# Two-layer model on one core: shift rows, prefetches and the fill of the routed attention regrouped

## The chip, the cores and the metric

The program runs on one core of one Trainium2 chip. TensorE (PE) does matrix products and transposes into PSUM, VectorE (DVE), ScalarE (ACT) and GpSimd (POOL) work on elements, SyncE (SP) issues DMAs. The metric is the device time of one execution in microseconds (us), and the figure shown is the median of several executions.

## The reference

The input is a batch of B = 8 sequences of S = 512 token numbers with a model width D = 192. The reference adds up five blocks on one residual stream: a token layer, a linear attention, a soft mixture of experts, a quantised attention, and a routed block (an attention and a mixture of eight experts). Both attentions that matter here have 12 heads of 16 numbers:

```python
# quantised attention
q, k, v = heads(fake_quant(x) @ fake_quant(w_qkv) + b_qkv)
attn = einsum('bhnd,bhmd->bhnm', fake_quant(q), fake_quant(k)) * hd ** -0.5
attn = fake_quant(softmax(attn, axis=-1))      # 8 bits, one scale for the whole tensor
out  = fake_quant(einsum('bhnm,bhmd->bhnd', attn, fake_quant(v))) @ fake_quant(w_proj) + b_proj
# the routed block's attention
attn = softmax(einsum('bhnd,bhmd->bhnm', q, k) * hd ** -0.5, axis=-1)
x    = x + einsum('bhnm,bhmd->bhnd', attn, v) @ proj_w + proj_b
```

The scale of a fake quantisation is the largest absolute value over 127. For `attn` it is the largest softmax value anywhere, so all row sums must be known before the first value can be rounded.

## The kernel before

The program is a list of stages, each a function that cuts its tiles out of one arena in SBUF: `embed_and_trace`, `linear_attention`, `soft_moe`, `quantised_attention`, `routed_attention`, `routed_experts`. A stage is a chain of `nc.Block`s. Inside a block every engine has its own written program, ordered by semaphores, and no engine leaves a block before all are through. Loops are either Python loops (the code is written out) or `Fori` loops that an engine turns itself. `Signal` is a semaphore with a count per batch; `Link` waits for the instruction just issued on its own engine.

Both attentions go over the scores twice, and both have a gap between the passes in which the shift of each row is made ready.

**Quantised attention.** The first pass (from L1616) forms per batch and head the scores of queries in rows, takes their maxima (`MXq`, L1658), and sums the exponentials (`RS`, L1673); 24 units of two row tiles per batch, on four pairs of PSUM banks. The block between the passes (L1680 to L1739) makes of sums and maxima one shift per row, `W_`: reciprocals of all sums and their maximum over all partitions (L1688, L1689, L1713), the logarithm (L1718), a multiply and subtract (L1694). `W_` is split into three bf16 parts in `BP`, batch by batch (L1698, L1703), transposed by 32 small transposes (L1728), copied to `BT` with 36 partitions (L1707), and each of its 36 partitions goes by a DMA of its own into a row of the query tile `QI` (L1738). `KI` has ones in the same rows, so the second pass's matmul subtracts the shift by itself. The second pass (L1742 on) needs K spread into `QM` and V in `VS`, two buffers by batch parity. SP asks for these after the rows have landed, four DMAs for K and one for V per batch (L1762, L1764). The second pass computes turned scores (L1781), exponentials (L1819), rounding (L1841) and the read-out (L1799).

**Routed attention.** To get fp32 accuracy out of bf16 products, Q and K are each split in three bf16 parts, and six pairs of parts are stacked in the contraction: `ST_[j][side]` has 6 x 16 = 96 rows (`KR`) and three more for the shift. The parts go to DRAM (`ra_parts`, L2100) and come back as stacks by 12 DMAs a batch (`load_stacks`, L2007 to L2012), two stack buffers by batch parity.
The first pass has a fill and then eight batches. The work on one batch's projections is cut into 14 `pieces` for TensorE: two `turn`s (L2117), eight `product`s (L2126), four `values` (L2136). The fill does all pieces of batches 0 and 1; after that every unit of scores of batch b (L2148) is followed by one piece of batch b + 2. ScalarE copies and splits, GpSimd subtracts (L2086, L2089), VectorE normalises rows (L2023) and takes the maxima of 24 units a batch (L2032). SP (L2093 to L2104) stores the parts of a batch and then loads its stacks as soon as the scores of the batch that held the buffer are through:

```python
for k in range(2):
    p2.wait(sp, b, k + 1)
    for n in range(3):
        dst = parts[bass.ds(b, 1)].rearrange("o k n f c s -> (o k) n c f s")[k, n]
        sp.dma_start(dst, PT[k][n]).then_inc(s_wr[k], 16)
prev(sp, u1, i, j)
for k in range(2):
    sp.wait_ge(s_wr[k], 16 * 3 * (b + 1) + 1)
    load_stacks(sp, b, j, ld[j], (k,))
```

The block between the passes (L2175 to L2211) negates the maxima (L2183), splits them in three parts (L2186, L2188) in a tile that GpSimd first fills with zeros (L2178), transposes (L2195), copies (L2203), and stores the rows to DRAM (`ra_shifts`, L2209). The second pass (L2213 on) loads per batch the stacks again, the shift rows from DRAM (L2233), and a copy of V (L2236). A batch is 12 steps: four score matmuls (L2250), two exponentials (L2313), four read-outs (L2288). After steps 1 and 3 TensorE projects a half of the batch before (L2263), which must wait for VectorE: copy of the read-out (L2347), shuffle, reciprocal, multiply (L2353).

## Time and profile before

| | |
|---|---|
| median of 3 executions | 2894.81 us (2891.12 to 2895.28) |
| profiled execution, its own time | 2868.81 us |
| its span | 2867.1 us |
| TensorE busy, share | 1967.8 us, 69% |
| VectorE busy, share | 1521.2 us, 53% |
| ScalarE busy, share | 1124.2 us, 39% |
| GpSimd busy, share | 312.9 us, 11% |
| mean granted TensorE clock | 0.768 of full |
| DMA, mean over the span | 88 GB/s |

The span is what the profile covers of its execution; 1.7 us of that execution's time lie outside it. The stages follow one another, so a share over the whole span mixes stages with different limits. The quantised first pass runs from about 1039 to 1335 us of the span, the second from 1386 to 1617; the routed first pass from 1674 to 1977 with its fill, the second from 2021 to 2271. The rows further down are places in time from these stretches.

### The profile page before, as it was taken

What the parts mean: (1) busy time and instruction counts of PE and PEld (TensorE: products, weight loads), DVE (VectorE), ACT (ScalarE), POOL (GpSimd) and SP (SyncE); (2) the same over time, 40 slices, a digit from 0 to 9 for tenths busy, and PEclk for the clock granted to TensorE, in tenths of its full rate; (3) what the DMA queues carried; (4) which work ended last, traced back from release to release, by engine and by line L of the source; (5) the groups of instructions that cost most, each with busy time, mean ns of one, the idle gap of its engine ahead of it and who ended that gap; (6) DMA issues with size and microseconds to landing.
All of it is one profiled execution on the core that took longest, in us unless ns stands there. A gap on an engine that the chain in (4) does not pass through costs nothing. (4 is left out here: it accounts for less than half of the span.)

```text
span 2867.1 us, 32319 instructions
## 1 busy us (share of the span) xinstructions
PE 1967.8 (69%) x9516; PEld 1035.9 (36%) x9538; DVE 1521.2 (53%) x2573; ACT 1124.2 (39%) x1862; POOL 312.9 (11%) x338
## 2 busy tenths in 40 slices
PE   4787788678873436664577648885799740999960
PEld 3645645353341100000111223321233340888850
DVE  4366378640026668886477738896477640111113
ACT  1102222231113579996588622220688410322210
POOL 4000000001110000000000042220000026000026
PEclk9899989777865655555799767775899755999985
DMA  3041100138930000000100048772898022455533
GB/s 71 11 137 39 42 17 22 54 146 311 411 151 11 0 15 11 11 11 2 36 26 29 1 77 114 105 105 30 117 111 109 3 95 79 174 200 209 202 105 107
DMA packets 140738, 251.39 MB, mean 88 GB/s; under 512 B 28762, under 2 KB 108251, under 8 KB 135628
## 3 DMA queue, kind: packets, MB, share of 16 engines
q1 hardware_dynamic: 128340, 225.99, 30.8%
q0 software_dynamic: 12304, 24.20, 2.9%
q8 instruction: 52, 0.85, 0.1%
q14 instruction: 42, 0.34, 0.0%
HBM read 194.69 MB, written 38.04 MB: 81 GB/s over the span
## 5 line engine op out<-in xcount | busy, mean ns | idle before, releaser
L1641 PE MATMUL ps<-arena 128*128 x376 | 194.3, 620 | 158.6 <-ACT ps L1673 96.0
L1673 ACT ACTIVATE ps<-ps,arena 128x512 f32<-128x512 f32 x384 | 291.8, 993 | 9.7 <-DVE arena L1652 9.7
L1658 DVE TENSOR_REDUCE arena<-ps 128x1024 f32 x192 | 234.4, 1224 | 47.9 <-PE ps L1641 46.5
L2032 DVE TENSOR_REDUCE arena<-ps 128x1024 f32 (+1 forms) x192 | 226.8, 1221 | 47.2 <-PE ps L2148 42.8
L1819 ACT ACTIVATE arena<-ps,arena 128x1024 f32<-128x1024 f32 x192 | 197.8, 1111 | 36.6 <-DVE arena L1841 27.3
L2313 ACT ACTIVATE arena<-ps 128x1024 f32<-128x1024 f32 x192 | 185.2, 1022 | 38.2 <-PE ps L2250 36.4
L2148 PE MATMUL ps<-arena 96*128 96x512 bf16 x384 | 159.7, 509 | 36.6 <-DVE arena L2032 23.6
L531 PE MATMUL ps<-arena 96*128 96x456 f32 (+1 forms) x512 | 176.5, 498 | 9.3 <-DMA arena<-arena 5.7
L2701 ACT ACTIVATE arena<-ps,arena 128x256 f32<-128x256 f32 x234 | 89.5, 481 | 235.9 <-PE ps L2666 235.9
L1841 DVE TENSOR_SCALAR arena<-arena 128x1024 bf16<-128x1024 f32 x192 | 130.8, 691 | 95.6 <-ACT arena L1819 79.0
L2718 DVE TENSOR_TENSOR arena<-ps,arena 128x384 f32<-128x384 f32 x39 | 21.7, 557 | 289.4 <-PE ps L2677 289.4
L1673 ACT ACTIVATION_READ_ACCUMULATOR ps<-ps,arena 128x1 f32 x384 | 171.6, 447 | 0.0
L2677 PE MATMUL ps<-arena 128*128 128x192 f32 x936 | 162.5, 331 | 0.7 <-DVE arena L2718 0.7
L2677 PEld LDWEIGHTS ps<-arena 128*128 128x128 f32 x936 | 151.0, 190 | 13.6 <-issue 13.6
L1781 PE MATMUL ps<-arena 128*128 (+1 forms) x370 | 117.3, 398 | 39.1 <-DMA arena<-arena 36.4
L1641 PEld LDWEIGHTS ps<-arena 128*128 128x128 bf16 x384 | 26.0, 112 | 326.3 <-ACT ps L1673 228.3
L2250 PE MATMUL ps<-arena 99*128 99x512 bf16 x384 | 103.2, 389 | 38.4 <-DMA arena<-arena 34.0
L531 PEld LDWEIGHTS ps<-arena 96*128 96x128 f32 x512 | 100.5, 205 | 76.6 <-issue 58.8
L2662 PE MATMUL ps<-arena 128*128 128x256 f32 x468 | 109.4, 384 | 0.9 <-ACT arena L2701 0.9
L1799 PE MATMUL ps<-arena 128*32 128x512 bf16 x384 | 77.5, 400 | 46.8 <-DVE arena L1841 38.6
L2288 PE MATMUL ps<-arena 128*32 128x512 f32 x768 | 103.5, 611 | 3.3 <-ACT arena L2313 3.3
L1204 DVE COPY arena<-ps 128x768 f32<-128x768 f32 x16 | 15.3, 957 | 159.9 <-PE ps L1246 159.9
(370 smaller groups left out, 3265.4 us busy)
## 6 DMA issues: line engine op xcount, KB each, us to landing
arena<-in_sm_w_dram SPq DMA_DIRECT2D x128, 576.0 KB
arena<-in_re_w_dram SPq DMA_DIRECT2D x39, 1252.0 KB, 5.7
arena<-ra_parts SPq DMA_DIRECT2D x192, 192.0 KB, 9.8
ra_parts<-arena SPq DMA_DIRECT2D x48, 192.0 KB, 2.5
routed_in<-arena SPq DMA_DIRECT2D x1, 7488.0 KB, 26.4
arena<-routed_in SPq DMA_DIRECT2D x39, 192.0 KB, 5.5
routed_out<-arena POOLq DMA_DIRECT2D x39, 192.0 KB, 2.3
arena<-la_xt SPq DMA_DIRECT2D x16, 384.0 KB, 3.3
```

Source lines behind the costliest of these rows:

```text
L531: ins = pe.matmul(ps[:, 2 * (t % 2) + bank, to:to + w], XTs[j][:, c, t * P:(t + 1) * P], Wx[:, kind, c, at:at + w], start=(c == 0), stop=( ...
L1641: ins = pe.matmul(ps[:, 2 * (n % 4) + t % 2, :], QM[j][:, h, t * P:(t + 1) * P], KI[:, b, h // HG, :], start=True, stop=True)
L1658: v.tensor_reduce(MXq[:, b, h, 2 * u:2 * u + 2], ps[:, 2 * (n % 4):2 * (n % 4) + 2, :], AX.X, ALU.max).then_inc(s_lk, 1)
L1673: ins = act.activation(bank, bank, ACT.Exp, bias=nb[n % 4][:, t % 2:t % 2 + 1], scale=c_exp, accum_out=RS[:, b, h, t:t + 1])
L1781: ins = pe.matmul(ps[:, 2 * (n % 3) + q, :], QM[j][:, h, c * P:(c + 1) * P], QI[:, bass.ds(b, 1), g, :].rearrange("p o s -> p (o s)"), sta ...
L1819: act.activation(PF[n % 2], ps[:, 2 * (n % 3):2 * (n % 3) + 2, :].rearrange("p a s -> p (a s)"), ACT.Exp, scale=c_exp).then_inc(pe_.sem, 1)
L1841: v.tensor_scalar(PB[n % 2], PF[n % 2], MAGIC, MAGIC, ALU.add, ALU.subtract).then_inc(rd.sem, 1)
L2032: v.tensor_reduce(MX[:, bass.ds(b, 1), 2 * (n % 2):2 * (n % 2) + 2, n // 2].rearrange("p o t -> p (o t)"), ps[:, 2 * (n % 2):2 * (n % 2) + ...
L2148: ins = pe.matmul(ps[:, t, :], ST_[j][0][0:KR, h, t * P:(t + 1) * P], ST_[j][1][0:KR, h, :], start=True, stop=True)
L2313: act.activation(PF[e // 2 % 2][:, 2 * (e % 2):2 * (e % 2) + 2, :], ps[:, 2 * (e % 3):2 * (e % 3) + 2, :], ACT.Exp, scale=HD ** -0.5).then ...
L2662: pe.matmul(unit(k), wr[:, k * P:(k + 1) * P], XT[j][:, 0, :], start=True, stop=False)
L2677: ins = pe.matmul(ps[:, 7, h * D:(h + 1) * D], HT[j][:, k, h * P:(h + 1) * P], wr[:, at:at + D], start=(k == 0), stop=(k == KH - 1))
```

## The change

Quantised attention. `RS` and `MXq` change their order to batch, row tile, head, and the heads are numbered so that the twelve heads of one partition group stand together (`at_head`). The largest reciprocal is formed as the reciprocal of the smallest sum. The split into parts is done for all batches at once, with the three parts innermost in `BP`. The copy to `BT` is divided: VectorE the first four batches, ScalarE the last four. Three parts of one head lie in neighbouring partitions of `BT` and go by one DMA, 12 instead of 36. SP asks for K and V of batches 0 and 1 at the start of the block between the passes.

Routed attention. The fill does the pieces of batch 0 alone; batch 0's units carry those of batches 1 and 2, two pieces after a unit; VectorE normalises batch 2 in the middle of batch 0's maxima. Maxima are written negated. After the loads of the last batch, SP loads the stacks of batch 0 for the second pass, once batch 6's scores are through. The block between the passes is gone: its work stands at the head of the second pass's block, without zero fill and negation, and shift rows go from `BT` straight into `ST_`, three DMAs a batch. V is read in place, so its copies and the DRAM tensor `ra_shifts` go. TensorE's and ScalarE's loops over the batches are written out, and the last two batches of VectorE's first pass become a loop.

```diff
-    RS, MXq = g3(P, [B, NH, T]), g3(P, [B, NH, T])
+    RS, MXq = g3(P, [B, T, NH]), g3(P, [B, T, NH])
+    VS = [OQ.rearrange("p g s -> p (g s)").rearrange("p (t h d) -> p t h d", t=T, h=NH),
+          g3(P, [T, NH, 32], BF16)]
+    at_head = lambda h: h % HG * NG + h // HG
...
-                                             scale=c_exp, accum_out=RS[:, b, h, t:t + 1])
+                                             scale=c_exp, accum_out=RS[:, b, t, at_head(h):at_head(h) + 1])
...
-    BP = g4(P, [B, T, 3, NH], BF16)
+    BP = TMP[:, S:S + 3 * B * T * NH // 2].bitcast(BF16).rearrange("p (n h k) -> p n h k", h=NH, k=3)
     BT = g4(3 * NH, [B, S], BF16)
-    W_ = TMP[:, 0:B * NH * T].rearrange("p (b h t) -> p b h t", b=B, h=NH)
+    W_ = TMP[:, 0:B * NH * T].rearrange("p (n h) -> p n h", h=NH)
+    rows = lambda a: a.rearrange("p b t h -> p (b t) h")
...
+    def spread(sp, b, j):
+
+        for q in range(HG):
+            sp.dma_start(QM[j][32 * q:32 * q + 32].rearrange("p (g j) s -> p g j s", j=HG)[:, :, q, :],
+                         KI[32 * q:32 * q + 32, b, :, :]).then_inc(km[j], 16)
+        sp.dma_start(VS[j], VI[:, b, :, :, :]).then_inc(km[j], 16)
...
-            l(v.reciprocal(W_, RS))
-            v.tensor_reduce(pmax, W_, AX.XYZ, ALU.max).then_inc(s_b, 1)
+            l(v.tensor_reduce(pmax, RS, AX.XYZ, ALU.min))
+            v.reciprocal(pmax, pmax).then_inc(s_b, 1)
...
             for k in range(3):
-                for b in range(B):
-                    ins = v.tensor_copy(BP[:, b, :, k, :], turned(W_, b))
-                    if b == B - 1:
-                        l(ins)
+                l(v.tensor_copy(BP[:, :, :, k], W_))
                 if k < 2:
-                    for b in range(B):
-                        ins = v.tensor_tensor(turned(W_, b), turned(W_, b), BP[:, b, :, k, :], ALU.subtract)
-                    l(ins)
+                    l(v.tensor_tensor(W_, W_, BP[:, :, :, k], ALU.subtract))
...
             v.wait_ge(s_bt, 1)
-            v.tensor_copy(BT.rearrange("p (u b) s -> p u (b s)", u=4),
-                          ps[0:3 * NH, 0:4, :].bitcast(BF16)).then_inc(s_bc, 1)
+            v.tensor_copy(BT[:, 0:4, :].rearrange("p (u b) s -> p u (b s)", u=2),
+                          ps[0:3 * NH, 0:2, :].bitcast(BF16)).then_inc(s_bc, 1)
...
+            act.wait_ge(s_bt, 2)
+            act.activation(BT[:, 4:8, :].rearrange("p (u b) s -> p u (b s)", u=2),
+                           ps[0:3 * NH, 2:4, :].bitcast(BF16), ACT.Copy).then_inc(s_bc, 1)
...
-                                       BP[:, b, t, :, :].rearrange("p k h -> p (k h)"), m.identb)
-            ins.then_inc(s_bt, 1)
+                                       BP[:, b * T + t, :, :].rearrange("p h k -> p (h k)"), m.identb)
+                if b % 4 == 3:
+                    ins.then_inc(s_bt, 1)
...
-            sp.wait_ge(s_bc, 1)
-            for k in range(3):
-                for h in range(NH):
-                    row = 32 * (h % HG) + HD + k
-                    sp.dma_start(QI[row:row + 1, :, h // HG, :], BT[k * NH + h:k * NH + h + 1, :, :]
-                                 ).then_inc(s_q, 16)
+            for j in range(2):
+                spread(sp, j, j)
+            sp.wait_ge(s_bc, 2)
+            for q in range(HG):
+                for g in range(NG):
+                    row, at = 32 * q + HD, 3 * (q * NG + g)
+                    sp.dma_start(QI[row:row + 3, :, g, :], BT[at:at + 3, :, :]).then_inc(s_q, 16)
...
-            sp.wait_ge(s_q, 16 * 3 * NH)
-            with sp.Fori(0, B // 2) as i:
+            with sp.Fori(1, B // 2) as i:
                 for j in range(2):
-                    b = 2 * i + j
                     prev(sp, av, i, j)
-                    for q in range(HG):
-                        sp.dma_start(QM[j][32 * q:32 * q + 32].rearrange("p (g j) s -> p g j s", j=HG)[:, :, q, :],
-                                     KI[32 * q:32 * q + 32, b, :, :]).then_inc(km[j], 16)
-                    sp.dma_start(VS[j], VI[:, b, :, :, :]).then_inc(km[j], 16)
+                    spread(sp, 2 * i + j, j)
...
-                        "p o t -> p (o t)"), ps[:, 2 * (n % 2):2 * (n % 2) + 2, :], AX.X, ALU.max).then_inc(mx.sem, 1)
-
-            def batch(b, ahead):
-                if ahead:
-                    norm(b + 2)
-                maxima(b, range(NU))
+                        "p o t -> p (o t)"), ps[:, 2 * (n % 2):2 * (n % 2) + 2, :], AX.X, ALU.max, negate=True
+                                    ).then_inc(mx.sem, 1)
 
             norm(0)
             norm(1)
-            with v.Fori(0, B - 2) as b:
-                batch(b, True)
-            batch(B - 2, False)
-            batch(B - 1, False)
+            maxima(0, range(6))
+            norm(2)
+            maxima(0, range(6, NU))
+            with v.Fori(1, B - 2) as b:
+                norm(b + 2)
+                maxima(b, range(NU))
+            with v.Fori(B - 2, B) as b:
+                maxima(b, range(NU))
...
+            u1.wait(sp, B - 2, NU)
+            load_stacks(sp, 0, 0, sl[0])
...
-            def batch(b, i, j, ahead):
-                pe.wait_ge(ld[j], 16 * NLD * (i + 1))
+            def batch(b, ahead):
+                pe.wait_ge(ld[b % 2], 16 * NLD * (b // 2 + 1))
+                rate = -(-len(ahead) // (NU - 2))
                 for n in range(NU):
-                    scores(b, j, n)
-                    if ahead and 0 < n <= len(pieces):
-                        piece, *which = pieces[n - 1]
-                        piece(b + 2, *which)
-
-            for b in range(2):
-                for piece, *which in pieces:
-                    piece(b, *which)
-            with pe.Fori(0, B // 2 - 1) as i:
-                for j in range(2):
-                    batch(2 * i + j, i, j, True)
-            batch(B - 2, B // 2 - 1, 0, False)
-            batch(B - 1, B // 2 - 1, 1, False)
-
...
-        def _(pool):
-            pool.memset(BPP, 0.0).then_inc(s_bz, 1)
-
-        @block.vector
-        def _(v):
-            l = Link(v, s_c)
-            l(v.tensor_scalar(M, M, -1.0, None, ALU.mult))
-            v.wait_ge(s_bz, 1)
-            for k in range(3):
-                l(v.tensor_copy(BP[:, :, k, :], M))
-                if k < 2:
-                    l(v.tensor_tensor(M, M, BP[:, :, k, :], ALU.subtract))
...
+                    scores(b, b % 2, n)
+                    if n:
+                        for to, (piece, *which) in ahead[rate * (n - 1):rate * n]:
+                            piece(to, *which)
+
+            for piece, *which in pieces:
+                piece(0, *which)
             for b in range(B):
-                for t in range(T):
-                    ins = pe.transpose(ps[:, b, 0:S // 2].bitcast(BF16)[:, t * P:(t + 1) * P],
-                                       BPP[:, b * T + t, :], m.identb)
-            ins.then_inc(s_bt, 1)
-
...
-            for b in range(B):
-                ins = act.activation(BT[:, b, :], ps[0:3 * NH, b, 0:S // 2].bitcast(BF16), ACT.Copy)
-            ins.then_inc(s_bc, 1)
-
-        @block.sync
-        def _(sp):
-            sp.wait_ge(s_bc, 1)
-            sp.dma_start(shifts.rearrange("b n s -> n b s"), BT).then_inc(s_sh, 16)
-            sp.wait_ge(s_sh, 16)
+                coming = {0: (1, 2)}.get(b, (b + 2,) if b + 2 < B else ())
+                batch(b, [(to, piece) for to in coming for piece in pieces])
...
-    VS = [g4(P, [T, NH, 2, HD]) for _ in range(2)]
     PF = [g4(P, [HG, S]) for _ in range(2)]
     OT, OS = g4(P, [NG, S]), g4(P, [NG, S])
+    BP, BT = g4(P, [B * T, 3, NH], BF16), g4(3 * NH, [B, S], BF16)
+    VT = V.rearrange("p b (t h n) -> p b t h n", t=T, h=NH)
...
+    NL2 = NLD + 3
...
-            with sp.Fori(0, B // 2) as i:
-                for j in range(2):
-                    b = 2 * i + j
-                    prev(sp, st, i, j)
-                    load_stacks(sp, b, j, sl[j])
-                    sp.dma_start(ST_[j][0][KR:KR + 3, :, :], shifts[bass.ds(b, 1)].rearrange(
-                        "o (k h) s -> (o k) h s", k=3)).then_inc(sl[j], 16)
-                    prev(sp, av, i, j)
-                    sp.dma_start(VS[j].rearrange("p t h k d -> p (t h k d)"),
-                                 V[:, bass.ds(b, 1), :].rearrange("p o n -> p (o n)")).then_inc(sl[j], 16)
+            def shift_rows(b):
+                for k in range(3):
+                    sp.dma_start(ST_[b % 2][0][KR + k:KR + k + 1, :, :], BT[NH * k:NH * k + NH, b, :]
+                                 ).then_inc(sl[b % 2], 16)
+
+            sp.wait_ge(s_b0, 1)
+            shift_rows(0)
+            shift_rows(1)
+            load_stacks(sp, 1, 1, sl[1])
+            sp.wait_ge(s_bc, 2)
+            for b in range(2, B):
+                prev(sp, st, b // 2, b % 2)
+                load_stacks(sp, b, b % 2, sl[b % 2])
+                shift_rows(b)
...
+            pe.wait_ge(s_c, 5)
+            turned = ps[0:3 * NH, 0:4, :].bitcast(BF16)
+            for b in range(B):
+                for t in range(T):
+                    at = b % 2 * S + t * P
+                    ins = pe.transpose(turned[:, b // 2, at:at + P],
+                                       BP[:, b * T + t, :, :].rearrange("p k h -> p (k h)"), m.identb)
+                if b in (1, 3, B - 1):
+                    ins.then_inc(s_bt, 1)
+            pe.wait_ge(s_b0, 1)
+            pe.wait_ge(s_bc, 2)
...
                         ins = pe.matmul(ps[32 * q:32 * q + 32, 6 + (j + g) % 2, :],
-                                        VS[j][:, c_, h, :, :].rearrange("p k d -> p (k d)"), PF[n % 2][:, q, :],
+                                        VT[:, b, c_, h, :], PF[n % 2][:, q, :],
...
-            batch(0, 0, 0, False)
-            with pe.Fori(0, B // 2 - 1) as i:
-                batch(2 * i + 1, i, 1, True)
-                batch(2 * i + 2, i + 1, 0, True)
-            batch(B - 1, B // 2 - 1, 1, True, False)
+            for b in range(B):
+                batch(b, b % 2, b > 0, b + 1 < B)
...
-            with act.Fori(0, B) as b:
+            act.wait_ge(s_bt, 3)
+            act.activation(BT[:, B // 2:B, :].rearrange("p (u b) s -> p u (b s)", u=2),
+                           ps[0:3 * NH, 2:4, :].bitcast(BF16), ACT.Copy).then_inc(s_bc, 1)
+            for b in range(B):
...
+            shift = Link(v, s_c)
+            for k in range(3):
+                shift(v.tensor_copy(BP[:, :, k, :], M))
+                if k < 2:
+                    shift(v.tensor_tensor(M, M, BP[:, :, k, :], ALU.subtract))
+            for u, done in enumerate((s_b0, s_bc)):
+                v.wait_ge(s_bt, u + 1)
+                v.tensor_copy(BT[:, 2 * u:2 * u + 2, :].rearrange("p b s -> p (b s)"),
+                              ps[0:3 * NH, u, :].bitcast(BF16)).then_inc(done, 1)
```

## Rows read from the trace of the kernel before

**Rows 1.** Window: busy PE, PEld, DVE, ACT, POOL; granted clock, DMA share, GB/s.
```profile
1352.00:1378.00 26.00, 0.00 (x0) 0.00 (x0) 0.00 (x0) 0.00 (x0) 0.00 (x0) 0.50 0.05 11
```

**Rows 2.** Timeline between the quantised passes, one row later: start, us, engine, line, operation.
```profile
1334.94 2.55 DVE L1688 RECIPROCAL arena<-arena 128x384 f32<-128x384 f32 x1 [3.71 <-PEq L1616]
...
1340.14 0.97 DVE L1698 CAST arena<-arena 128x48 bf16<-128x48 f32 x8
...
1341.14 1.26 DVE L1703 TENSOR_TENSOR arena<-arena 128x48 f32<-128x48 f32 x8
...
1349.46 2.28 DVE L1707 COPY arena<-ps 36x4096 bf16<-36x4096 bf16 x1 [3.76 <-PE ps L1728]
...
1351.77 26.02 SPq L1738 DMA_DIRECT2D arena<-arena  x36
...
1379.40 3.08 SPq L1762 DMA_DIRECT2D arena<-arena  x4
...
1385.80 2.34 PE L1781 MATMUL ps<-arena 128*128 128x512 bf16 x5 [36.38 <-DMA arena<-arena]
...
1618.97 0.16 DVE L1355 RECIPROCAL arena<-arena 128x1 f32<-128x1 f32 x1
```

**Rows 3.** Timeline between the two passes of the routed attention.
```profile
1976.95 3.67 DVE L2183 TENSOR_SCALAR arena<-arena 128x384 f32<-128x384 f32 x1 [0.41 <-PEq L2014]
...
1980.66 0.36 DVE L2186 CAST arena<-arena 128x384 bf16<-128x384 f32 x1
...
1981.05 0.56 DVE L2188 TENSOR_TENSOR arena<-arena 128x384 f32<-128x384 f32 x1
...
1983.05 3.60 PE L2195 MATMUL ps<-arena 128*128 128x128 bf16 x32 [7.76 <-DVE arena L2186]
...
1986.68 3.95 ACT L2203 ACTIVATE arena<-ps 36x512 bf16<-36x512 bf16 x8 [77.22 <-PE ps L2195]
...
2002.62 19.21 SPq L2012 DMA_DIRECT2D arena<-ra_parts  x12
...
2020.67 2.74 PE L2250 MATMUL ps<-arena 99*128 99x512 bf16 x6 [34.02 <-DMA arena<-arena]
...
2023.11 3.77 ACT L2313 ACTIVATE arena<-ps 128x1024 f32<-128x1024 f32 x4
```

**Rows 4.** Timeline of the first pass's fill and of its batch 0.
```profile
1679.18 9.87 PE L2126 MATMUL ps<-arena 97*96 97x512 f32 x16 [1.62 <-ACT arena L2056]
...
1693.25 3.98 DVE L2023 TENSOR_SCALAR arena<-arena 128x192 f32 x4 [14.41 <-PE ps L2117]
...
1717.60 1.89 PE L2148 MATMUL ps<-arena 96*128 96x512 bf16 x4 [9.16 <-DMA arena<-ra_parts]
...
1725.32 24.24 DVE L2032 TENSOR_REDUCE arena<-ps 128x1024 f32 x20 [1.26 <-PE ps L2148]
...
1727.16 0.60 PE L2148 MATMUL ps<-arena 96*128 96x512 bf16 x2
...
1727.59 1.02 PE L2126 MATMUL ps<-arena 96*96 96x512 f32 x2
...
1728.45 0.59 PE L2148 MATMUL ps<-arena 96*128 96x512 bf16 x2
...
1748.37 5.65 SPq L2012 DMA_DIRECT2D arena<-ra_parts  x12
```

**Rows 5.** Timeline of the first pass's last units.
```profile
1969.48 7.07 DVE L2032 TENSOR_REDUCE arena<-ps 128x2 f32<-128x1024 f32 x6
```

**Rows 6.** Timeline of batch boundaries in the second pass.
```profile
2048.55 1.28 ACT L2313 ACT_TABLE_LOAD   x1
...
2078.13 1.28 ACT L2313 ACT_TABLE_LOAD   x1
...
2085.22 2.22 PE L2263 MATMUL ps<-arena 128*128 128x192 f32 x12 [0.69 <-DVE arena L2353]
...
2107.71 1.28 ACT L2313 ACT_TABLE_LOAD   x1
```

More of the change, by code:

```diff
@@ L1769, in _ @@
             av.start(pe)
-            pe.wait_ge(s_q, 16 * 3 * NH)
+            pe.wait_ge(s_q, 16 * NG * HG)
             def unit(n):
@@ L1946, in routed_attention @@
     ps, ra = m.ps, m.wk[1]
-    parts, shifts = io.ra_parts, io.ra_shifts
+    parts = io.ra_parts
     sem = lambda name: SEMS.new(nc, name)
@@ L2004, in routed_attention @@
     ld = [sem(f"ra_stacks{j}_loaded") for j in range(2)]
+    sl = [sem(f"ra_q_k_shift{j}_loaded") for j in range(2)]
     NLD = 2 * len(PAIRS)
     def load_stacks(eng, b, j, done, sides=(0, 1)):
+        one = slice(b, b + 1) if isinstance(b, int) else bass.ds(b, 1)
         for k in sides:
             for n, pair in enumerate(PAIRS):
-                src = parts[bass.ds(b, 1)].rearrange("o k n f (j d) s -> (o k) n d (f j) s", d=HD)[k, pair[k]]
+                src = parts[one].rearrange("o k n f (j d) s -> (o k) n d (f j) s", d=HD)[k, pair[k]]
                 eng.dma_start(ST_[j][k][HD * n:HD * n + HD, :, :], src).then_inc(done, 16)
@@ L2215, in routed_attention @@
     PF = [g4(P, [HG, S]) for _ in range(2)]
     OT, OS = g4(P, [NG, S]), g4(P, [NG, S])
+    BP, BT = g4(P, [B * T, 3, NH], BF16), g4(3 * NH, [B, S], BF16)
+    VT = V.rearrange("p b (t h n) -> p b t h n", t=T, h=NH)
+    M = MX.rearrange("p b t h -> p (b t) h")
+    s_c, s_bt, s_b0, s_bc = (sem(f"ra_shift_{n}") for n in ("chain", "turned", "first_copied", "copied"))
     NS = NG * T
@@ L2221, in routed_attention @@
     s_l3 = sem("ra_out_chain")
-    sl = [sem(f"ra_q_k_v{j}_loaded") for j in range(2)]
-    NL2 = NLD + 2
+    NL2 = NLD + 3
     with nc.Block(no_gpsimd_drain=True) as block:
@@ L2265, in project, with batch @@
                 ins.then_inc(pr.sem, 1)
-            def batch(b, i, j, behind, ahead=True):
+            def batch(b, j, behind, ahead=True):
                 for n in range(NS):
```

30 lines of the change are left out of this document (7 added, 23 removed).

## Prediction, made before the changed kernel was run

> **What bounds the kernel now.** I read the page first. Its chain that ended last covers only 2% of the span, so it says nothing here. The 40 slices say more: the busy digits and the granted clock sink together between the quantised passes and again between the routed passes, so these are two places where hardly anybody is at work. I then took windows and the timeline around both, SP's own timeline for the DMA queue, and last the boundaries between batches inside the passes.
>
> First gap, between the quantised passes: VectorE starts at 1334.94 and the first score of the second pass at 1385.80, 50.9 us in a row of single steps [rows 2]. The window shows every engine at zero for 26 us, TensorE's clock at its lower level (0.50), while SP issues 36 one-row DMAs, with the DMA engines 5% busy [rows 1]: the cost is the issuing, not the bytes. Only when the last row has landed does SP ask for K and V of the next pass, another 6.4 us (1379.40 to 1385.80) [rows 2].
>
> Second gap, between the routed passes: the last maxima end at 1976.55 [rows 5], the first exponential starts at 2023.11 [rows 3]. The sums before SP may ask for anything take until 1990.6, then the shift rows go out to DRAM, then the stacks come in; TensorE waits 34.0 us for a DMA [rows 3].
>
> Inside the routed first pass VectorE sets the pace: 1.21 us a unit of 1024 maxima, 24 units a batch [rows 4]. Its fill ends at 1717.60, when TensorE has been waiting 9.16 us for the stacks of batch 0, not for its own work [rows 4]. In the second pass a batch takes 29.58 us (2078.13 to 2107.71) [rows 6].
>
> **The change, part by part.** Sums are made in the profiled execution: 2868.81 us, with a span of 2867.1. The median shown is 2894.81, 26.0 higher. The edits take out waits and instructions of fixed length, so I subtract the same microseconds from the median; scaling them by 1.009 would move half a microsecond.
>
> *Quantised gap.* (a) The reciprocal of all 384 sums (2.55) becomes a minimum, at the price of the maximum it replaces, and a reciprocal of one element (0.16): 2.4 less [rows 2]. The logarithm moves up with it, to 1336.4; its table load of 1.28 (the length in [rows 6]) starts with the gap and is over by 1336.2. (b) Split into parts: 24 casts and 16 subtractions in groups of eight, 3 x 0.97 and 2 x 1.26, 5.6 with gaps [rows 2], become three casts and two subtractions of 384 elements. The routed stage has just these at 0.36 and 0.56 [rows 3], so 2.35; written with a step of three elements perhaps 0.1 more each. Gain 2.5 to 3.2, taken 2.9. (c) The 2.28 copy out of PSUM is halved. VectorE's half lies under the transposes; ScalarE's half, 36x2048, starts when they end. Eight copies of 512 take 3.95 [rows 3], 0.49 each, so at most 1.98: 0.3 less. (d) Rows: 36 DMAs in 26.02, 0.72 each; 12 are 8.7, or 9.2 at the 0.77 of the K spreads (3.08 for 4) [rows 2]. 17.3 less. Each now carries three partitions. If only three DMA engines serve such a DMA, each gets 96 KB. Of the old transfers 288 packets kept 16 engines busy 5% of 26 us, 0.072 us a packet [rows 1]; 96 packets on one engine are 6.9 us, still under the issuing, and only the last one's tail grows by 0.5. So 16.8; if a packet costs twice that, 13.8 us on three engines, it is 11.7. The Trainium skill, in "DMA: Bandwidth & Descriptors", section on why a DMA increments its semaphore by 16, says that the engine count is the largest up to 16 that divides the slowest dimension of both sides: eight before, three now. No row here shows which engines were used; this rule speaks against the edit and is the reason for the 0.5. (e) K and V of batches 0 and 1 are now asked for at the gap's start: 8 x 0.77 and 2 x 0.6 of SP's time, over by about 1342, and SP isn't wanted until about 1346. 6.4 less. What hides it is VectorE's and TensorE's chain of 11 us; without that cover it costs 7.4. The landing time of the last row, 1.6 (1377.79 to 1379.40) [rows 2], stays. Sum of (a) to (e): 28.8, bounds 23 to 30.
>
> *Short fill.* Before, the 14 pieces of batch 1 (2 transposes, 8 products, 4 of values) ran while the stacks of batch 0 were on their way, and TensorE still waited 9.16 us. Their removal from the fill makes nothing earlier: SP's stores and loads of batch 0 depend on batch 0 alone. The first score stays at 1717.6. But now these pieces come into batch 0, two to a unit. A pair of score matmuls is 0.43 (1727.16 to 1727.59), a product piece 0.86 (1727.59 to 1728.45) [rows 4]. Before, a unit was 1.29, near VectorE's 1.21, and the scores of batch 0 were done when SP asked again at 1748.37, 30.8 us [rows 4]. After: unit 0 is 0.9, units 1 to 14 are 14 x (0.43 + 2 x 0.86) = 30.1, units 15 to 23 are 9 x 1.21 = 10.9, and the first four units at half clock (1.89 for four matmuls at the start [rows 4]) add 1.6: 43.5. Turns and values are lighter than products; the two waits for ScalarE behind a transpose fill that up. So 12.7 later, and no later batch has slack to win it back. The stacks of batch 1: in the fill, from the last product (1679.18 + 9.87 = 1689.05) to their use took 28.5 us [rows 4]. Its products now end near 1731, so 1759.5, just inside the 1761 at which batch 0 ends. What is late next, if they miss it, is batch 1 itself, by 1 to 4 us. The normalisation of batch 2 now falls where GpSimd subtracts, and in such a place it took 3.98 for four [rows 4]: up to 2.7 more. I take 13, bounds 9 to 19. Negated maxima cost nothing in the reduction. Batches 6 and 7 go into a loop: 1.212 a unit in the loop, 1.178 out of it (24.24/20, 7.07/6) [rows 4, 5], 48 x 0.034 = 1.6 more.
>
> *Routed gap.* The negation (3.67, beside a memset of GpSimd's that goes too) leaves 2.4 of casts and subtractions, to 1979.4. The transposes take 3.6 [rows 3], to 1983.0. ScalarE's half of the copy, 1.95 at most, to 1985.0. VectorE copies the first two batches' quarter from about 1980.5, in some 0.6; three row DMAs of batch 0 follow at SP's 0.47 (5.65/12) [rows 4], issued by 1982.7, landed at the 1.6 of [rows 2] by 1984.3, at 4 us by 1986.7. Stacks of batch 0 are asked for when batch 6's scores end, 24 units of 1.178 or 28 us before the gap [rows 5]; the slowest issue of such a load here took 19.2, with another in front of it [rows 3]. The load of batch 1's stacks starts near 1984 behind six row DMAs and lands near 2001; it is wanted 27 us after the start. So the first score is at 1985.0 for 2020.67, and the table load no longer stands behind it, 1.3 less: the exponential at 1986.5 for 2023.11. 36.6 less, bounds 33 to 37.
>
> *Loops written out.* ScalarE's loop reloads its table once a batch, 1.28 [rows 6]; seven go. But TensorE cannot pass the projection of the batch before, and that waits for VectorE (0.69 idle at 2085.22, released by L2353) [rows 6], whose chain of copy, shuffle, reciprocal and multiply starts at the last read-out and does not see the table. ScalarE and TensorE come 1.28 earlier to a wait of 0.69, which becomes 1.97. Gain 0; if none of that held, 9. The Trainium skill, "ScalarE: Activation LUTs", section on what ACT_TABLE_LOAD costs, gives 1283 ns and a drain, 2.66 us a switch: the trace agrees on the load, shows no drain ahead of it, and by that price the most would be 18.6.
>
> Sum: -28.8 + 13 + 1.6 - 36.6 = -50.8. 2868.8 becomes 2818.0, and the median 2894.8 becomes 2844.0.
>
> **Rivals.** *The fill is free:* the stacks of batch 0 land sooner without batch 1's work beside them, or ScalarE's and VectorE's share sets the pace. For it: DMA and engines did run together there. Against: those loads were a plain transfer with nothing of batch 1 in front. Sum -63.8: 2831. *The table loads count:* -59.8, 2835. Against: the projection wait. *Something new waits:* rows on three engines 5, stacks of batch 1 missing their time 4, the GpSimd collision 2.7; together -39: 2856. *The prefetch doesn't get through:* batch 0 of the second routed pass waits for its stacks as before; 19 us of the 36.6 are lost, 2863. The stacks' buffer is free at batch 6's end, so I see nothing for it. *Slower than before:* TensorE's code for both routed passes is now written out, 16 batches. If reading it held TensorE up, under a DMA load that fills these stages, the change would turn at 50.8/16 = 3.2 us a batch; at 5 us it would end at 2924. Against: TensorE's old loop turns at every second batch, and its neighbouring batches take the same 29.58 (2048.55 to 2078.13 to 2107.71) [rows 6], so nothing shows that reading code costs; no row prices it for straight code.
>
> **How the numbers follow.** Forecast as summed 0.55, free fill 0.10, table loads 0.10, new waits 0.15, prefetch lost 0.05, slower 0.03, elsewhere 0.02. The likeliest case alone spans 2836 to 2852 by its bounds; with the neighbours the range is 2828 to 2860. A difference under 0.2% (6 us) can't be told from none: faster 0.95, same 0.02, slower 0.03.
>
> **What would show it.** From the last exponential of the first quantised pass to the first score of the second: about 22 us, with 12 row DMAs in 9. The first routed score after the fill as late as before, after a TensorE wait of 26 us, and batch 0 some 43 us long. From the last maxima to the first exponential about 10 us. A second-pass period still 29.6, with TensorE's wait ahead of L2263's projection near 2. I am wrong if batch 0 stays near 31, if the period falls to 28.3, or if either gap keeps a wait for a DMA of more than 3 us.

## Result and profile after

The changed kernel takes 2853.39 us (median of 4 executions, 2846.80 to 2857.18), the kernel before 2894.06 beside it: 40.7 us less, ratio 0.9859, 95% interval 0.9838 to 0.9879. The forecast, 2844.0, was 9 us too low; its range, 2828 to 2860, holds the time. The profiled executions are 2868.81 us before and 2854.61 after. Their difference is too small by 26 us, because that of before was 25 us under its median, in stages that the change doesn't touch: the quantised gap began at 1334.94 in it and at 1346.25 in that of after, and from the last exponential to the end it took 611.5 us and then 624.4. The change isn't the reason: in the changed kernel's later trace, beside which the kernel before took 2869.69 us, the two are 1335.26 and 609.3, and that execution takes 2828.48 us, 40.3 under the profiled one of before. So I compare stretch by stretch.

| stretch | before | after | difference | forecast |
|---|---|---|---|---|
| quantised gap: VectorE's start to first score of the second pass | 50.86 | 24.07 | -26.8 | -28.8 |
| quantised second pass and the way to the routed fill | 289.81 | 291.78 | +2.0 | 0 |
| routed fill: first transpose to first score | 41.99 | 42.55 | +0.6 | 0 |
| routed first pass: first score to last maxima | 258.95 | 276.03 | +17.1 | +14.6 |
| routed gap: last maxima to first exponential | 46.56 | 10.24 | -36.3 | -36.6 |
| routed second pass: first to last exponential | 232.46 | 237.58 | +5.1 | 0 |
| sum | | | -38.3 | -50.8 |

The sum lies within the interval of the difference of the medians, which is 35 to 47 us. The second row, on which the forecast has no word, is small and steady: 291.7 to 292.3 us in all ten traces here with the quantised part of the change, 289.8 and 290.1 in the two without it. Its cause is open. A stretch of one trace is not exact, the routed first pass least of all: with the same code it took 271.3 to 276.0 us in six traces.

The timeline of after in the quantised gap, which answers to [rows 2]:

```profile
1346.20 2.66 SPq L1693 DMA_DIRECT2D arena<-arena  x4
1346.20 1.28 ACT L1726 ACT_TABLE_LOAD   x1 [0.32 <-PEq L1619]
1346.25 0.55 DVE L1701 TENSOR_REDUCE arena<-arena 128x1 f32<-128x384 f32 x1 [3.72 <-PEq L1619]
...
1349.07 0.49 DVE L1710 CAST arena<-arena 128x384 bf16<-128x384 f32 x1
...
1349.59 0.56 DVE L1712 TENSOR_TENSOR arena<-arena 128x384 f32<-128x384 f32 x1
...
1355.21 1.87 ACT L1728 ACTIVATE arena<-ps 36x2048 bf16<-36x2048 bf16 x1 [6.90 <-PE ps L1739]
1357.10 9.76 SPq L1752 DMA_DIRECT2D arena<-arena  x12
...
1370.32 1.91 PE L1786 MATMUL ps<-arena 128*128 128x512 bf16 x4 [15.15 <-DMA arena<-arena]
```

The work up to the copy's end (1357.08) takes 10.8 us for 16.8, as forecast (6.0 less for 5.6). From there to the first score 13.2 us pass, and the forecast has 10.8: 8.7 of issuing (12 x 0.72, since its 17.3 is 26.02 less 8.7), 0.5 and 1.6 for the tail. The twelve rows take 9.8, 0.81 each, and from the last issue (1366.86) to the first score it is 3.5. These 2.4 less the 0.4 gained before are the miss of 2.0.

The timeline of the fill and batch 0, the routed first pass, against [rows 4]:

```profile
1685.23 5.79 SPq L2019 DMA_DIRECT2D arena<-ra_parts  x12
...
1704.65 1.89 PE L2157 MATMUL ps<-arena 96*128 96x512 bf16 x4 [26.09 <-DMA arena<-ra_parts]
```

TensorE waits 26.09 us where it waited 9.16, the forecast's 26, and the first score is no earlier. Its own rows go on:

```profile
1709.87 3.70 PE L2135 MATMUL ps<-arena 97*96 97x512 f32 x4 [0.77 <-ACT arena L2063]
...
1714.21 3.02 PE L2135 MATMUL ps<-arena 97*96 97x512 f32 x4
1717.07 0.59 PE L2157 MATMUL ps<-arena 96*128 96x512 bf16 x2
1717.50 1.88 PE L2135 MATMUL ps<-arena 97*96 97x512 f32 x4
1719.22 0.59 PE L2157 MATMUL ps<-arena 96*128 96x512 bf16 x2
...
1753.13 1.89 PE L2157 MATMUL ps<-arena 96*128 96x512 bf16 x4 [3.33 <-DMA arena<-ra_parts]
```

From 1717.07 a unit with two pieces is the forecast's 2.15 (1717.07 to 1719.22). Before that products run in 3.70 and 3.02 instead of 1.88: after 26 us of idleness TensorE starts at the lower of its clock levels (the granted clock from 1704.65 to 1717.07 is 0.52, where 0.50 is 1.2 GHz). Batch 0's scores end at 1749.8, 45.1 us after the first for the 43.5 forecast, and then TensorE waits 3.33 for the stacks of batch 1. SP's row for these:

```profile
1732.21 5.99 SPq L2019 DMA_DIRECT2D arena<-ra_parts  x12
```

From 1732.21 to their use is 20.9 us. The collision of batch 2's normalisation with GpSimd did not come: its four instructions took 1.24 us together.

So batch 0 takes 48.5 us in this trace, but this is the longest of six. Its window here, and in the run with the table loads back, whose first pass is the same code:

```profile
1704.65:1753.13 48.48, 40.44 (x129) 18.23 (x129) 31.07 (x32) 16.69 (x28) 16.79 (x8) 0.78 0.55 83
1703.31:1746.02 42.71, 36.03 (x129) 17.21 (x129) 29.50 (x28) 16.70 (x28) 16.80 (x8) 0.90 0.59 94
```

The work is the same, the granted clock is 0.78 here and 0.90 there, and the wait for the stacks of batch 1 is 3.3 us here and 0.9 there. Batch 1 took 31.0 us here for 34.0 before, and the forecast had allowed no later batch to win anything back.

Batches 6 and 7, whose maxima are now in VectorE's loop, took 60.7 us (1919.94 to 1980.68) for 57.7 (1918.89 to 1976.55). Their units:

```profile
1951.12 19.60 DVE L2039 TENSOR_REDUCE arena<-ps 128x1024 f32 x16 [0.18 <-PE ps L2157]
```

That is 1.225 us a unit (19.60/16) for the 1.178 of [rows 5] out of the loop. The negation isn't the reason: in the kernel before, too, such units start 1.14 and 1.32 us apart by turns in the loop and 1.14 and 1.21 out of it.

The timeline of the routed gap, for [rows 3]:

```profile
1981.35 0.36 DVE L2305 CAST arena<-arena 128x384 bf16<-128x384 f32 x1 [0.67 <-PEq L2021]
...
1983.74 3.60 PE L2219 MATMUL ps<-arena 128*36 128x128 bf16 x32 [4.43 <-DVE arena L2305]
1984.89 1.46 DVE L2310 COPY arena<-ps 36x1024 bf16<-36x1024 bf16 x2 [1.21 <-PE ps L2219]
1985.60 5.08 SPq L2196 DMA_DIRECT2D arena<-arena  x6
...
1987.38 1.87 ACT L2289 ACTIVATE arena<-ps 36x2048 bf16<-36x2048 bf16 x1 [76.88 <-PE ps L2219]
...
1989.26 1.28 ACT L2295 ACT_TABLE_LOAD   x1
...
1989.87 3.57 PE L2232 MATMUL ps<-arena 99*128 99x512 bf16 x8 [2.54 <-DMA arena<-arena]
...
1990.92 3.77 ACT L2295 ACTIVATE arena<-ps 128x1024 f32<-128x1024 f32 x4 [0.38 <-PE ps L2232]
```

The stacks have come; what TensorE waits 2.54 us for are the shift rows of batch 0, at 0.85 us an issue (5.08/6) instead of the 0.47 taken.

The second pass is where the forecast of nothing failed. TensorE's timeline at the first two boundaries, for [rows 6]:

```profile
2023.27 3.83 PE L2245 MATMUL ps<-arena 128*128 128x192 f32 x12 [1.86 <-DVE arena L2344]
...
2030.92 2.22 PE L2245 MATMUL ps<-arena 128*128 128x192 f32 x12
...
2054.61 2.22 PE L2245 MATMUL ps<-arena 128*128 128x192 f32 x12 [1.86 <-DVE arena L2344]
...
2060.59 1.73 PE L2245 MATMUL ps<-arena 128*128 128x192 f32 x9
```

The wait grew from 0.69 to 1.86, near the 1.97 forecast, at every boundary. But behind it the same twelve matmuls take 3.83 us once and 2.22 another time, and to the next projection it is 7.65 or 5.98 us. The windows behind the two waits (the columns of [rows 1]) show why:

```profile
2023.27:2031.00 7.73, 7.73 (x37) 4.50 (x37) 2.89 (x6) 3.34 (x4) 0.00 (x0) 0.78 1.15 122
...
2054.61:2060.60 5.99, 5.99 (x37) 2.92 (x37) 3.03 (x6) 3.27 (x4) 0.00 (x0) 1.00 1.16 127
```

The granted clock, the column after the five engines, is 0.78 behind the first wait, which mixes both levels (1.2 and 2.4 GHz), and 1.00 (2.4 GHz) behind the second. In this profile three of seven boundaries are of the slow kind: ScalarE is idle 5.68 us in them and 4.00 in the others. 3 x 1.68 = 5.0 is the +5.1. Before, with a wait of 0.69, the clock stayed at 1.00.

### The profile page after: what moved, and what is told of

Its sections match the earlier page's. It is cut to its first block and busy times, and to the rows that moved or that the text cites. A ratio compares the mean times of both kernels' runs of the same rounds, so it can differ in the third digit from the quotient of the medians.

```text
span 2852.9 us, 31531 instructions
## 1 busy us (share of the span) xinstructions
PE 1960.8 (69%) x9516; PEld 1034.2 (36%) x9538; DVE 1512.6 (53%) x2539; ACT 1115.3 (39%) x1849; POOL 307.2 (11%) x337
```

## Experiments

Each ratio is to the kernel before on the same chip, whose medians were 2870.54 for the first four, 2891.78 for the next four and 2869.69 for the last two. Where an expectation names microseconds, it mostly counts from the changed kernel's 2853 beside a kernel before of 2894; on a chip where the kernel before takes 2870 the ratio is what to compare. The theory after the result: the missing ten microseconds are row DMAs and their landing (2), the short fill (2.5) and TensorE's lower clock in the second pass (5).

**The old fill in the changed kernel** (VectorE's loop over batches with it; TensorE's part is shown):

```diff
-            for piece, *which in pieces:
-                piece(0, *which)
+            for b in range(2):
+                for piece, *which in pieces:
+                    piece(b, *which)
             for b in range(B):
-                coming = {0: (1, 2)}.get(b, (b + 2,) if b + 2 < B else ())
+                coming = (b + 2,) if b + 2 < B else ()
```

> The changed kernel with the old fill: all 14 pieces of batches 0 and 1 before the first score, one piece a unit after that. Theory: the short fill alone made the first routed pass longer (from first score to last maxima 276.0 us in the changed kernel, 259.0 before). Then the first score stays about 42.3 us after the first transpose, batch 0 lasts 31 to 32 instead of 48.5 us, there is no wait of 3.3 us for the stacks of batch 1, and the time is some 16 us under the changed kernel, near 2837. Rival: the loops written out or the vector engine's new loop are to blame, and the first pass stays at 274 to 276 us, the time at 2853.

Measured: 2815.77 us, ratio 0.9801 (0.9787 to 0.9814), 0.0058 or 16.8 us of 2894 better than the changed kernel; with both intervals that is 10 to 24. The first pass took 260.2 us for 276.0. Its first score:

```profile
1696.37 1.89 PE L2154 MATMUL ps<-arena 96*128 96x512 bf16 x4 [10.72 <-DMA arena<-ra_parts]
```

The wait in front is 10.72 us: the work in the fill lay in the shadow of the transfer. The short fill is a loss. Over all traces here its first pass averages 273.8 us (six), that of the changed kernel's loops with the old fill 261.5 (three: this one and the two runs with both edits below): 12.3 us, so 276.0 against 260.2 is the upper end of the price. Batches 6 and 7 stay at 60.2 us in each of these three, so VectorE's loop costs 2.6 us of its own and the forecast had 1.6.

**The projection later.** Moved from after steps 1 and 3 to after steps 2 and 3, so that VectorE's chain has a step more.

```diff
-                    if behind and n in (1, 3):
-                        project(b - 1, 1 - j, n // 2)
+                    if behind and n in (2, 3):
+                        project(b - 1, 1 - j, n - 2)
```

> The changed kernel with the two halves of the projection after steps 2 and 3 of the next batch instead of 1 and 3. Theory: in the second routed pass the wait for the vector engine's chain sets the period (29.6 us with and without table loads), 1.86 us of TensorE waiting at each boundary, and after three of seven such waits the granted clock fell to half for the projection. One step (1.96 us) later the wait is over: period 28.0 to 28.6, no projection at half clock, 8 to 12 us less than the changed kernel, near 2843. Rival: ScalarE's exponentials set the period and the wait only moves to the second half or to the bank of the read-outs: period 29.3 to 29.6, gain under 3 us.

Measured: 2809.60 us, ratio 0.9785 (0.9772 to 0.9799). The second pass fell from 237.6 to 220.2 us, 17.4 less and more than expected. TensorE's waits before the projection are 0.31 us at most. Two windows of 192 us over most of the second pass show what has gone. The changed kernel's:

```profile
2021.00:2213.00 192.00, 178.98 (x1054) 65.70 (x1051) 132.77 (x182) 144.38 (x150) 0.00 (x0) 0.97 0.64 72
```

The window of the kernel with the later projection:

```profile
2008.00:2200.00 192.00, 190.10 (x1156) 65.69 (x1148) 146.20 (x200) 158.31 (x164) 0.00 (x0) 1.00 0.64 72
```

TensorE is busy 190.1 of 192 us, at a granted clock of 1.00: now it is the bound. What the 17.4 are made of is taken apart by the last runs.

**ScalarE's loop written out in the kernel before**, nothing else:

```diff
-            with act.Fori(0, B) as b:
+            for b in range(B):
```

> The kernel before with one edit: ScalarE's loop over the batches of the second routed pass written out, so seven table loads of 1.28 us go. Theory: they lay beside the wait for the vector engine. From first to last exponential the pass stays at 232.5 us, or gets up to 5 us longer where TensorE's longer wait (0.69 becomes 1.9) lets the granted clock fall; against the kernel before 0.999 to 1.002. Rival: the loads were on the path, 9.0 us less, 0.997.

Measured: 2872.77 us, ratio 1.0006 (0.9997 to 1.0016). The seven loads of 1.28 us are gone and nothing is won: by the ratio it is 1.7 us more, with an interval from 0.9 less to 4.6 more. Its boundaries are those of the changed kernel, of both kinds:

```profile
2051.82 2.22 PE L2263 MATMUL ps<-arena 128*128 128x192 f32 x12 [1.85 <-DVE arena L2353]
...
2081.43 3.54 PE L2263 MATMUL ps<-arena 128*128 128x192 f32 x12 [1.86 <-DVE arena L2353]
```

So the slower boundaries, four of seven here, come from this edit: in its trace the second pass is 238.3 us for 232.5. That the executions as a whole got slower by it is not shown, since the interval holds 1.

**The quantised part alone** in the kernel before (its diff as shown for that attention).

> The kernel before with the quantised attention's part of the change alone. Theory: its gap shrinks from 50.9 to about 24.1 us, as in the changed kernel, 26.8 less, and nothing else moves: 0.9907 of before, 2867. Rival: part of that is given back later, because the clock or the transfers behind it differ: under 22 us.

Measured: 2844.11 us, ratio 0.9907 (0.9892 to 0.9922), 26.4 us less, beside the 26.8 of the stretch with its 2.4 us more behind it (292.2 for 289.8). This part does alone what it does in the whole change, the small loss behind the gap included.

**Old fill and later projection together.**

> The changed kernel with both edits, the old fill (first pass 16 us shorter in its trace) and the projection after steps 2 and 3 (second pass 17 to 21 us shorter). Theory: the two lie in different passes and add. Ratios so far, against the kernel before on the same chip: 0.9801 and 0.9785, with the changed kernel at 0.9859 on its own chip; together 0.9785 - 0.0058 = 0.973, near 2792 where before is 2870. Rival: a pass that starts earlier loses what it gained at its first stacks or at the clock: 0.977 or more.

Measured: 2822.04 us, ratio 0.9751 (0.9730 to 0.9771), between the two numbers, and the interval holds both. The trace decides for adding up: the first pass takes 262.2 us, 13.8 less than in the changed kernel, and the second 220.1, 17.5 less. These 31.3 us make 0.9751 of 0.9859; the expected 0.973 was too low because it took 16.8 for the fill.

**The same, with the rows from two queues:** six of the twelve row DMAs are issued by ScalarE; the calls are shown.

```diff
+            act.wait_ge(s_bc, 2)
+            place_rows(act, (2, 3))
...
             sp.wait_ge(s_bc, 2)
-            for q in range(HG):
-                for g in range(NG):
-                    row, at = 32 * q + HD, 3 * (q * NG + g)
-                    sp.dma_start(QI[row:row + 3, :, g, :], BT[at:at + 3, :, :]).then_inc(s_q, 16)
+            place_rows(sp, (0, 1))
```

> The kernel of the run above, and the twelve three-row DMAs of the quantised gap issued half by SP and half by ScalarE. They take 9.7 us of issuing from SP alone, 0.81 each, and the last row is usable about 3 us after its issue. Theory A, each DMA's issue sets the pace: two queues need 4.9, the first score of the second quantised pass follows about 8 us after the copies in place of 12.8, 4.9 us less. Theory B, few DMA engines carry all rows and are the limit (96 packets each at 0.072 us or more, 6.9 us or more, and a tail): 9 to 12 us, so 1 to 4 us less. Against the run above 0.998 to 1.000.

Measured: 2818.48 us, ratio 0.9736 (0.9714 to 0.9757), the fastest version here against its own kernel before; its interval overlaps that of the run before it, the trace decides:

```profile
1355.33 4.92 SPq L1702 DMA_DIRECT2D arena<-arena  x6
1355.33 5.80 ACTq L1702 DMA_DIRECT2D arena<-arena  x6
...
1364.31 2.32 PE L1792 MATMUL ps<-arena 128*128 128x512 bf16 x5 [10.92 <-DMA arena<-arena]
```

From the end of the copy to the first score 9.0 us, 12.9 in the run before it. The issue takes 5.8 for 9.8, since ScalarE needs longer for its six (5.80) than SP (4.92), and the tail behind the last issue stays at 3.2 (3.1 in the run before). The 3.9 us are fewer than theory A's 4.9 and within theory B's 1 to 4, so the number alone doesn't part them; that the first score follows the end of the issuing by the same time in both speaks for A. The tail has a part of each. In the changed kernel's trace the semaphore updates, which no view prints, put the landing of the first of the twelve 2.1 us behind its issue and of the last 3.0; the one-row DMAs of before landed 1.3 us behind theirs, first and last alike. So 0.9 us of the tail is growth over the twelve; why a single row of three partitions takes 0.8 longer than one of one is open.

**The table loads back in the changed kernel:** only ScalarE's loop as before.

> The changed kernel with ScalarE's loop over the batches of the second routed pass kept as a loop, so that a table load of 1.28 us comes back seven times (TensorE's code stays written out). Theory: TensorE then waits 0.7 us instead of 1.9 for the vector engine before the projection, and its granted clock does not fall there: no projection at half clock, every batch boundary with ScalarE idle 2.8 us beside a load of 1.28, and from first to last exponential 231 to 233 us instead of the 237.6 of the changed kernel: 5 us less in spite of the added work. Rival: written-out code of TensorE itself costs those 5 us, or the loads are on the path after all: 237 to 246 us.

Measured: 2847.85 us, ratio 0.9842 (0.9821 to 0.9862), which overlaps with the changed kernel's interval. In the trace the second pass took 233.2 us for 237.6. ScalarE's rows at two boundaries:

```profile
2041.83 1.28 ACT L2295 ACT_TABLE_LOAD   x1
2043.12 5.65 ACT L2295 ACTIVATE arena<-ps 128x1024 f32<-128x1024 f32 x6
2051.68 3.90 ACT L2295 ACTIVATE arena<-ps 128x1024 f32<-128x1024 f32 x4 [2.91 <-PE ps L2232]
...
2071.40 1.28 ACT L2295 ACT_TABLE_LOAD   x1
2072.69 5.65 ACT L2295 ACTIVATE arena<-ps 128x1024 f32<-128x1024 f32 x6
2081.25 3.90 ACT L2295 ACTIVATE arena<-ps 128x1024 f32<-128x1024 f32 x4 [2.91 <-PE ps L2232]
```

With seven loads of 1.28 us more the pass is shorter: every boundary is of the fast kind, TensorE's wait is 0.77, and its projection takes 2.22. An eighth load stands before the first exponential and makes the gap 1.4 us longer (11.6 for 10.2), so 3.0 of the 4.4 us are left. The pass is also within 0.7 us of the 232.5 of before, so TensorE's written-out code costs no more than that.

**Without the early ask for batch 0's stacks:** the load goes out at the head of the gap.

```diff
-            u1.wait(sp, B - 2, NU)
-            load_stacks(sp, 0, 0, sl[0])
...
+            load_stacks(sp, 0, 0, sl[0])
             sp.wait_ge(s_b0, 1)
```

> The changed kernel without the one early step: the stacks of batch 0 for the second routed pass are asked for at the head of the gap, where SP is free, instead of during batch 7 of the first pass. Theory: 12 loads under no other load need 16 to 17 us from the first issue, and the row DMAs follow them in the queue: first score about 18 us after the gap's start instead of 8.5, 9 to 11 us more than the changed kernel. Rival (the forecast's price for a lost prefetch): 19 us more. Rival: nothing, since the shift rows set the moment.

Measured: 2867.51 us, ratio 0.9908 (0.9889 to 0.9926), 14 us more than the changed kernel. From the end of ScalarE's copy to the first exponential 16.2 us instead of 1.7. Timeline:

```profile
1990.59 13.00 SPq L2019 DMA_DIRECT2D arena<-ra_parts  x12
...
2003.13 3.15 PE L2231 MATMUL ps<-arena 99*128 99x512 bf16 x7 [17.03 <-DMA arena<-arena]
```

The load was issued from 1979.79 and the score stood until 2003.13, 23.3 us, with batch 1's stacks issued in between; the early ask works, and is worth 14 to 15 us, between the 9 to 11 and the 19 named for it. The 9 to 11 had counted 16 to 17 us for the load; it took 23.3.

**The changed kernel again, and the later projection with the table loads back.** Two runs on one chip, to take the 17.4 us apart.

> The changed kernel as it is, beside the next run on the same chip, as the measure for it. Expected ratio to the kernel before 0.986, as measured for it, within 0.002. In its second routed pass some of the seven boundaries show a wait of TensorE for VectorE of 1.86 us and then the projection's twelve matmuls in more than 3 us instead of 2.22; if the granted clock decides by chance of timing, the number of such boundaries may differ from the three seen before.

> The changed kernel with two edits: the projection of the batch before is put behind the third and fourth step of the next batch instead of the second and fourth, and ScalarE's loop of the second routed pass is a loop again, so its table load of 1.28 us stands in each batch. It tells apart where the 17.4 us of the later projection came from. Theory A: the projection's wait was the only cover of the table loads, and with the wait gone they count in full; the period goes from 27.9 to 29.2, the second pass from 220.2 to about 229, ratio 0.9785 + 0.0031 = 0.982. Theory B: the later projection moves the end of the batch for another reason and something else still covers the loads: period 27.9, ratio within 0.001 of 0.9785. In both no projection runs at the lower clock.

Measured: 2830.84 us, ratio 0.9863 (0.9848 to 0.9878), and 2817.96 us, ratio 0.9822 (0.9808 to 0.9836), which is theory A's 0.982; its interval keeps theory B's 0.9785 out. In the trace of the changed kernel five of seven boundaries were of the slow kind this time, and its second pass took 241.0 us. ScalarE's rows of the other:

```profile
2004.36 1.28 ACT L2295 ACT_TABLE_LOAD   x1
...
2015.33 1.94 ACT L2295 ACTIVATE arena<-ps 128x1024 f32<-128x1024 f32 x2 [2.07 <-PE ps L2232]
...
2033.16 1.28 ACT L2295 ACT_TABLE_LOAD   x1
...
2044.13 1.94 ACT L2295 ACTIVATE arena<-ps 128x1024 f32<-128x1024 f32 x2 [2.07 <-PE ps L2232]
```

Periods are 28.8 us and the pass 225.7. So from 237.6 or 241.0 us: the clock's share is what the loads back alone give, 4.4 to 7.8; putting the projection later gives 7.5 more (233.2 to 225.7); only then do the loads count, 5.5 us (225.7 to 220.2), 0.8 a batch and not theory A's full 1.28. By traces the loads cost 6.9 us with the 1.4 in the gap; the ratios say 10.6, and their intervals allow 5 to 16.

## Why the prediction came out as it did

The signs and the places were right: two gaps gained, one price paid. What was off were sizes, and one term taken at nothing, which is a step that failed although the time lies in the range.

- *Quantised gap, -28.8: measured -26.8.* (a) to (c) were right within 0.4 us. (d) took 0.72 a row in its sum (8.7 for the twelve) where it is 0.81, and a tail of 1.6 + 0.5 where it is 3.5. As (d) assumed, issuing is the larger part of the time: dividing it between two queues gave 3.9 us. (e) held: nothing of K and V is late. The sign "a wait for a DMA of more than 3 us in either gap" came true by the letter (15.15 us here), but the forecast's own sum has 10.8 us of rows in that wait, so as a sign it was badly made.
- *Quantised second pass, no term: measured +2.0,* in every trace with this part of the change.
- *Short fill and loop, +13 + 1.6: measured +17.1, +0.6 in the fill.* Of the 17.1 batches 6 and 7 have 3.1, where the loop's 1.6 was taken from a mean of units (1.212 and 1.178) that the loop's own units of 1.225 exceed. Batches 0 to 5 have 14.0, near the 13, but by luck in this trace: batch 0 was 5.0 too long (1.6 in the scores, mostly the start at half clock, for which the sum has 1.6 already, and 3.3 for the stacks of batch 1, "just inside", a lateness that the text names as 1 to 4 and didn't add), and batches 1 to 5 gave 3.6 back, which "no later batch has slack" excludes. Over six traces the 13 holds better than in the one (12.3), and the stacks are late by 0.3 to 3.3.
- *Routed gap, -36.6: measured -36.3.* The early ask carries 14.5 of it.
- *Loops written out, 0: measured +5.1, and +8.5 in the later trace.* That the loads were hidden was right: 1.0006 without them. The step "a wait of 0.69, which becomes 1.97. Gain 0" forgot what a longer wait does to TensorE's clock. The rival "the table loads count" is refuted in this kernel; they count after the projection has been moved.
- *Rivals.* The fill was not free. "Something new waits", 2856, lies nearer to 2853.4 than the forecast does; of its three parts the rows (2) and the stacks (3.3) came, GpSimd's did not, and the clock was not among them. The prefetch got through. Code written out on TensorE cost at most 0.7 us in the second pass (233.2 for 232.5 with the loads back).
- *Sum, -50.8: measured -38.3 by stretches, -40.7 by medians:* 2.0 + 2.0 + 3.1 + 0.3 + 5.1 = 12.5 us of misses, all of one sign. The largest one comes from the term that had a bound for a gain and none for a loss. That the time still lies in the range owes something to the room that the range left for the neighbours, of which "something new waits" was the nearest; the clock in the second pass was in none of them.

The Trainium skill, "DMA: Bandwidth & Descriptors", section on why a DMA increments its semaphore by 16, would have three engines serve such a row, where it has eight for the old one. The trace agrees. The packets while the 36 old rows were under way, and while the 12 new ones were:

```profile
DMA packets 577, 0.30 MB, mean 11 GB/s; under 512 B 288, under 2 KB 576, under 8 KB 576
...
DMA packets 324, 0.30 MB, mean 23 GB/s; under 512 B 36, under 2 KB 324, under 8 KB 324
```

Beside the same 288 packets of 1 KB there are 288 small ones for 36 DMAs and 36 small ones for 12, so eight and three for each. By that section of the Trainium skill every engine that takes part ends with one write to the semaphore. The window of the new rows, with columns as in [rows 1]:

```profile
1358.00:1369.00 11.00, 0.00 (x0) 0.00 (x0) 0.00 (x0) 1.20 (x1) 0.00 (x0) 0.50 0.13 27
```

A share of 0.13 is 2.1 of 16 engines, or 0.7 of three: near their limit, but not at it.

The Trainium skill, "ScalarE: Activation LUTs", section on what ACT_TABLE_LOAD costs, gives 2.66 us for a switch to a different set of functions. The loads in the second pass bring the exponential's again, so their 0.8 us a batch doesn't test that price. A load for another function stands at 1346.20 above: 1.28 us, with 0.32 us of idleness ahead, and the logarithm starts at 1347.69, 0.2 us behind it. So this trace doesn't show the drain either, and the measurement decides.

## What to carry to other kernels

Before taking work out of a fill, look at what the engine waits for at its end: where that is a transfer that needs none of the work, the work is free there and is paid in full inside the batches, with the start at the lower clock on top. Work that is hidden behind a wait gives nothing when removed, and the longer wait may cost; move the waiting instruction back first and then remove (here the second pass fell from 232.5 us to 225.7 by the first and to 220.2 by both). Asking early for the next pass's data gave 14.5 us, and 12 larger row DMAs in place of 36 took 9.8 us to issue for 26.0. And look at more than one trace before you split a difference of a few microseconds: one stretch with the same code varied by 5 us here.

## What the runs showed of the hardware

TensorE's granted clock fell to 0.50 (1.2 GHz) behind waits of 1.86 us for VectorE in three to five of seven otherwise equal boundaries, 21 of 35 in five traces, and its twelve fp32 matmuls then took 3.3 to 3.9 us for 2.22; behind waits of 0.69 to 0.78, 21 in three traces, it never fell. The same 1.28 us table load, put back, lowered the second pass by 4.4 us. DMAs of 24 KB on three partitions took 0.81 us each to issue and landed 2.1 us behind the issue at first and 3.0 at the end of twelve, those of 8 KB on one partition 0.72 and 1.3; the first left three small packets each beside their data, the second eight. VectorE's maxima of 1024 elements took 1.225 us a unit in its own loop and 1.178 written out.
